# Masked copies of v made by four DMAs within SBUF, pooled residual on GpSimd, and a TensorE loop that begins with the convolution

## Chip, core and metric

One core of one Trainium2 chip. The metric is the device time of the whole program in microseconds, the median of several runs.

## What is computed

`x` is 4 x 128 x 96 x 96 in f32. It is group-normalised (32 groups of 4 channels) and goes through a windowed linear attention over windows of 4 x 4 pixels; the result is added to `x`.

```python
qkv = jnp.einsum('nchw,oc->nohw', xw, qkv_w)        # xw: windows of the normalised x
pooled = _avg_pool5(qkv)                            # 5x5 mean, zero padding, within a window
msq = jnp.concatenate([qkv, pooled], axis=1)
msq = msq.reshape(N, -1, 3 * DIM, ws * ws).transpose(0, 1, 3, 2)
q = jax.nn.relu(msq[..., :DIM])
k = jax.nn.relu(msq[..., DIM:2 * DIM])
v = msq[..., 2 * DIM:]
v = jnp.pad(v, ((0, 0), (0, 0), (0, 0), (0, 1)), constant_values=1.0)
kv = jnp.einsum('ngld,nglm->ngdm', k, v)
out = jnp.einsum('ngld,ngdm->nglm', q, kv)
out = out[..., :-1] / (out[..., -1:] + 1e-15)
y = jnp.einsum('nchw,oc->nohw', out, proj_w)        # after going back to image order
y = y * inv[None, :, None, None] + (bn_beta - bn_mean * inv)[None, :, None, None]
x = x + y
```

## The kernel before

**Tiling.** All of `x` stays in SBUF (`x_all`, channels on the partitions). A strip is four image rows, 384 pixels, 24 windows; there are 96 strips (`NS`), 24 per image. Each strip goes through every stage twice: in full (16 pixels per window) and pooled (a 5x5 mean within a 4x4 window has only 9 different values, so 216 columns per strip).

**GpSimd (POOL)**, lines 226 to 279: `normalise_and_pool(s, p)` writes the normalised strip in window order to `xn[:, p]` (L255 subtracts the mean, L256 multiplies by the inverse deviation, signal `xn_ready`) and eight adds through the helper at L234 make the pooled sums `xp[:, p]` (`xp_ready`). Strip s+2 is made in step s, once TensorE has done `conv_q(s)` (semaphore `q_p`), which frees the buffer.

**TensorE (PE)**, lines 528 to 669. One step of the loop is, in this order: `kv_products` full, `kv_products` pooled (both L582, small 64x32 tiles of the array), `conv_q` (L556 full, L558 pooled), `conv_kv` of the next strip (L538, pixels stationary), `transposes` of the last strip's output (L627), `conv_kv_pooled` of the next strip (L549), `project` of the last strip (L633, L635), `out_products` full and pooled (both L611, small tiles). Step 0 and step 95 are written out; steps 1 to 94 are a hardware loop (`pe.Fori`) of 47 turns with two steps in its body. The program begins each step with `kv_products`, so the jump back lies between the pooled `out_products` and the full `kv_products`.

**ScalarE (ACT)**, lines 281 to 364. A step is `relu_q`, `relu_q_pooled`, `relu_k(s+1)` (L286), `to_image(s-1)` (L325), `pooled_out(s-1)` (L332), `masked_v(s+1)` full (L305, four copies of v, each scaled by a column of 0 and 1 so that only one window's rows are left), `relu_k_pooled(s+1)` (L292), `masked_v(s+1)` pooled (L305, six copies).

**VectorE (DVE)**, lines 366 to 526. A step is `own_heads` full and pooled (L446), the statistics of a later image in some steps (L377), `residual(s-1)` (L452 adds the full part of y and the shift to `x_all`; L462, four adds, spreads the pooled y over the 16 pixels of each window; signal `y_done`), `divide` full and pooled (L472, L473, L476). The pooled `kv_products` waits for `vm_p`, the last of the six pooled masks; the full `kv_products` for `km_f`, `vm_f` and `y_done`.

**SyncE (SP)** issues the loads and, for each strip, waits for `y_done` and issues the store (L222).

Of the kernel before, what the change touches and what calls it, by code (L numbers as in the profile page):

```python
# [8 lines left out]
ALU = mybir.AluOpType  # L9
ACT = mybir.ActivationFunctionType  # L10

P = 128
# [23 lines left out]
C_VF = C_OWN + QG * KC  # L36
C_VP = C_VF + EF
# [5 lines left out]
def constants():  # L43


    c = np.zeros((P, N_CONST), np.float32)
    p = np.arange(P)
    c[:, C_IDENT:C_IDENT + P] = np.eye(P)
    quad, head = p // Q4, p % Q4 // D
    for j in range(QG):  # L50
        at = C_OWN + j * KC
        c[:, at:at + KC] = (quad[:, None] % QG == j) & (head[:, None] == np.arange(KC)[None] // HC)
    win_f, win_p = p % Q4 // PX, p % Q4 // PXP
    side = np.array([1, 2, 1])
    times = (side[:, None] * side[None]).ravel()[p % Q4 % PXP][:, None]
    own_f = (quad % QG * WF + win_f)[:, None] == np.arange(EF)[None]
    own_p = ((quad % QG * WP + win_p)[:, None] == np.arange(EP)[None]) & (win_p < WP)[:, None]
    c[:, C_VF:C_VF + EF] = own_f
    c[:, C_VP:C_VP + EP] = own_p * times / 25.0
    c[:, C_TP:C_TP + EP] = own_p * times  # L60
    pads = p % Q4 >= WP * PXP
    c[np.concatenate([p[~pads], p[pads]]), C_PACK + p] = 1
    return c


def build(nc, x, wq, wkv, proj, bn, consts, out):
# [20 lines left out]
    with ExitStack() as ctx:  # L87
# [29 lines left out]
        xn = sb("xn", [2, SP])  # L117
        hs = sb("hs", [NW, WS, NP])
# [5 lines left out]
        vm_full = sb("vm_full", [TF, EF, 4, KC])  # L124
        vm_pool = sb("vm_pool", [TP, EP, 4, KC])
# [8 lines left out]
        o_sb = sb("o_sb", [SP + SPP])  # L134

# [33 lines left out]
        vm_f, vm_p = sem("vm_f"), sem("vm_p")  # L169
        qm_f, qm_p = sem("qm_f"), sem("qm_p")  # L170
# [7 lines left out]
        added_f = sem("added_f")  # L178
        y_done = sem("y_done")
# [30 lines left out]
        def _(sp):  # L210
# [7 lines left out]
            for b in range(B):  # L218
                for t in range(SPB):

                    sp.wait_ge(y_done, t + (b * SPB + 2))
                    sp.dma_start(out_v[:, b, bass.ds(t * SP, SP)],  # L222
                                 x_all[:, bass.ds(t * SP + b * HW, SP)]).then_inc(stored, 16)
# [3 lines left out]
        def _(pool):  # L227
# [3 lines left out]
            pool.memset(q_pool[:], 0.0).then_inc(pads_zero, 1)  # L231

# [3 lines left out]
            def normalise_and_pool(s, p):  # L236


                xr = xn[:, p].rearrange("p (w r c) -> p r w c", r=WS, c=WS)
                xv = xn[:, p].rearrange("p (w r c) -> p w r c", r=WS, c=WS)  # L240
                xo = xp[:, p].rearrange("p (q j) -> p q j", j=Q4)[:, :, 0:WP * PXP].rearrange(
                    "p q (w r c) -> p q w r c", w=WP, c=NP)
                h3 = hs[:].rearrange("p (q w) r c -> p q w r c", w=WP)
# [8 lines left out]
                src = x_all[:, bass.ds(s * SP, SP)].rearrange("p (r w c) -> p r w c", r=WS, c=WS)  # L252
# [6 lines left out]
                link(add(ht[:], xv[:, :, :, 1], xv[:, :, :, 2]), 2)  # L259
                link(add(hs[:, :, :, 0], ht[:], xv[:, :, :, 0]), 3)  # L260
                add(hs[:, :, :, 2], ht[:], xv[:, :, :, 3])
                link(add(hs[:, :, :, 1], hs[:, :, :, 0], xv[:, :, :, 3]), 4)
# [3 lines left out]
                add(xo[:, :, :, 1, :], xo[:, :, :, 0, :], h3[:, :, :, 3, :]).then_inc(xp_ready, 1)  # L266

            def step(s, b, at, phase):
                if s < NS - 2:
# [3 lines left out]
                    normalise_and_pool(s + 2, s % 2)  # L273

            pool.wait_ge(pads_zero, 3)
# [3 lines left out]
            over_strips(step)  # L279

        @block.scalar
        def _(act):
# [12 lines left out]
            def masked_v(s, pooled):  # L295

                ready, free, done, bank, vm, tiles, wins, mask = (
                    (v_p, kv_p, vm_p, V_P, vm_pool, TP, EP, C_VP) if pooled else
                    (v_f, kv_f, vm_f, V_F, vm_full, TF, EF, C_VF))
                act.wait_ge(ready, s + 1)  # L300
                wait(act, free, s)
                heads = vm[:].rearrange("p t e i (h c) -> p t e (i h) c", c=HC)
                src = ps[:, bank, 0:tiles * P].rearrange("p (t h m) -> p t h m", t=tiles, m=D)
                for e in range(wins):
                    last = act.activation(heads[:, :, e, :, 0:D], src, ACT.Copy, scale=col(mask + e))  # L305
                last.then_inc(done, 1)
# [26 lines left out]

            def square_root(n):
# [6 lines left out]
            act.wait_ge(pads_zero, 3)  # L341

            def step(s, b, at, phase):
                relu_q(s)
                relu_q_pooled(s)
                if not is_last(s):
                    relu_k(s + 1)
                if not is_first(s):
                    to_image(s - 1)
                    pooled_out(s - 1)  # L350
                if not is_last(s):
                    masked_v(s + 1, False)
                    relu_k_pooled(s + 1)
                    masked_v(s + 1, True)
# [4 lines left out]
            masked_v(0, False)  # L359
            relu_k_pooled(0)  # L360
            masked_v(0, True)
            over_strips(step)
            to_image(NS - 1)
            pooled_out(NS - 1)

        @block.vector
        def _(dve):
# [48 lines left out]

            dve.memset(dev[:], 0.0).then_inc(y_done, 1)
# [31 lines left out]
            def residual(s):  # L449
# [4 lines left out]
                dve.wait_ge(y_p, s + 1)  # L454
                dve.wait_ge(added_f, s + 1)
                src = ps[:, Y_P, 0:SPP].rearrange("p (w r c) -> p w r c", r=NP, c=NP)
                dst = xs.rearrange("p (r w c) -> p w r c", r=WS, c=WS)
                ends, ends_p, mid, mid_p = slice(0, WS, WS - 1), slice(0, NP, NP - 1), slice(1, 3), slice(1, 2)
                for rows, rows_p in ((ends, ends_p), (mid, mid_p)):
                    for cols, cols_p in ((ends, ends_p), (mid, mid_p)):  # L460
                        part = dst[:, :, rows, cols]
                        last = dve.tensor_tensor(part, src[:, :, rows_p, cols_p].to_broadcast([P, NW, 2, 2]),  # L462
                                                 part, ALU.add)
                last.then_inc(y_done, 1)
# [53 lines left out]
            for vm, wins, mask in ((vm_full, EF, C_VF), (vm_pool, EP, C_TP)):  # L518
                for e in range(wins):
                    ones = vm[:, :, e].rearrange("p t i (h c) -> p t (i h) c", c=HC)[:, :, :, D]  # L520
                    last = dve.tensor_copy(ones, col(mask + e).unsqueeze(2).to_broadcast(list(ones.shape)))
# [7 lines left out]
        def _(pe):  # L529
# [12 lines left out]
            def conv_kv_pooled(s, p):  # L542
                pe.wait_ge(xp_ready, s + 1)

                wait(pe, qm_f, s)
# [16 lines left out]
            def kv_products(s, pooled):  # L562


                k, vm, tiles, wins, bank, done = (
                    (k_pool, vm_pool, TP, EP, KVP, kv_p) if pooled else (k_full, vm_full, TF, EF, KVF, kv_f))
                pe.wait_ge(km_p if pooled else km_f, s + 1)
                pe.wait_ge(vm_p if pooled else vm_f, s + 1)
                if pooled:

                    wait(pe, num_f, s)
                else:

                    wait(pe, y_done, s)

                pe.nop(nofuse=True)
                n = wins * KC
                for t in range(tiles):
                    for r in range(G):
                        rows = slice(H64 * r, H64 * (r + 1))  # L580
                        for i in range(4):
                            last = pe.matmul(ps[Q4 * i:Q4 * (i + 1), bank + r, t * n:(t + 1) * n],  # L582
                                             k[rows, t, Q4 * i:Q4 * (i + 1)], vm[rows, t, :, i, :],
                                             start=True, stop=True)
                last.then_inc(done, 1)

            def out_products(s, pooled):


                q, kvc, done, bank, tiles, wins = (  # L590
                    (q_pool, kvc_pool, out_p, OUTP, TP, WP) if pooled else
                    (q_full, kvc_full, out_f, OUTF, TF, WF))
                pe.wait_ge(qm_p if pooled else qm_f, s + 1)
                pe.wait_ge(kvc_p if pooled else kvc_f, s + 1)
                if not pooled:

                    pe.wait_ge(kvc_p, s + 1)
                elif not is_last(s):

                    pe.wait_ge(km_f, s + 2)  # L600
                    pe.wait_ge(vm_f, s + 2)
                pe.nop(nofuse=True)
                n = QG * KC
                blocks = q[:].rearrange("p n e j -> p n (e j)")
                for t in range(tiles):
                    for e in range(wins):
                        for g in range(G):
                            rows = slice(H64 * g, H64 * (g + 1))
# [88 lines left out]
```

## Time and profile before

| | us |
|---|---|
| median of 3 runs | 930.72 (928.78 to 931.36) |
| the profiled execution's own time | 930.24 |
| its span, first to last instruction | 928.3 |
| TensorE matmul busy | 873.8 |
| weight load busy | 733.4 |
| VectorE busy | 772.3 |
| ScalarE busy | 609.5 |
| GpSimd busy | 456.0 |
| mean granted TensorE clock | 0.993 of full speed |

Busy time is the union of an engine's instructions. The ends of matmuls are modelled, so on TensorE the distance from one start to the next says more than the busy time. "issue" as a releaser means that the engine waited for nothing that the profile shows.

### The profile page before, as it was taken

The numbers are of one execution on the slowest core, as the hardware profiler recorded it, in microseconds if no ns is written. First come the engines' busy times: TensorE is split into PE (matmuls) and PEld (weight loads), VectorE is DVE, ScalarE is ACT, GpSimd is POOL, SyncE is SP. The second block draws the span as 40 slices with busy tenths as digits, with TensorE's granted clock in tenths as the row PEclk, the third lists the DMA queues.
The fourth block names the chain that finished last, engine by engine and source line by source line (L and its number), as shares of the span: only waits on it lengthen the run. The fifth ranks groups of instructions, "written<-read, shape, count | busy, mean of one in ns | idle before, by whom it ended". The sixth has DMA issues, their size and how long they took to land.

```text
span 928.3 us, 65376 instructions
## 1 busy us (share of the span) xinstructions
PE 873.8 (94%) x29282; PEld 733.4 (79%) x29282; DVE 772.3 (83%) x1625; ACT 609.5 (66%) x1542; POOL 456.0 (49%) x967
## 2 busy tenths in 40 slices
PE   0689999999999999999999999999999999999997
PEld 0578888888888888888888888888888888888885
DVE  7369989998878898998878998999887878787886
ACT  0457676767676767676766667676767676767673
POOL 1545454545454545555554545454545454545550
PEclk9999999999999999999999999999999999999998
DMA  9910000000000000000000000000000000000000
GB/s 378 431 50 17 26 17 26 17 26 17 25 19 25 26 17 26 17 26 17 26 17 26 18 26 17 26 17 27 17 26 17 25 25 18 26 17 26 18 26 27
DMA packets 15893, 38.77 MB, mean 42 GB/s; under 512 B 1888, under 2 KB 14688, under 8 KB 15456
## 3 DMA queue, kind: packets, MB, share of 16 engines
q1 hardware_dynamic: 15840, 38.26, 10.6%
q14 instruction: 44, 0.36, 0.1%
q8 instruction: 9, 0.15, 0.1%
HBM read 19.38 MB, written 18.87 MB: 41 GB/s over the span
## 4 chain that ended last, share of the span: by engine, by line
PE 93%; issue 3%; DVE 2%; POOL 1%; DMA 0%; ACT 0%; DVEq 0%; POOLq 0%
PE ps L611 23%; PE ps L582 19%; PE ps L538 14%; PE ps L549 9%; PE ps L556 9%; PE ps L633 7%; PE ps L627 6%; PE ps L635 4%; PE ps L558 4%; DVE stats L377 1%; DMA x_all<-x 0%; POOL hs L234 0%; DVE kvc_full L446 0%; POOL xp L234 0%; ACT o_sb L325 0%
## 5 line engine op out<-in xcount | busy, mean ns | idle before, releaser
L255 POOL TENSOR_TENSOR xn<-x_all,mean_t 128x384 f32<-128x384 f32 x96 | 79.4, 827 | 393.6 <-PE ps L558 375.1
L305 ACT ACTIVATE vm_pool<-ps,cst 128x256 f32<-128x256 f32 x576 | 225.5, 543 | 0.4 <-PE ps L549 0.4
L446 DVE TENSOR_TENSOR kvc_full<-ps,cst 128x864 f32<-128x864 f32 x192 | 193.7, 1050 | 17.8 <-PE ps L582 17.6
L446 DVE TENSOR_TENSOR kvc_pool<-ps,cst 128x864 f32<-128x864 f32 x192 | 193.2, 1048 | 0.0
L305 ACT ACTIVATE vm_full<-ps,cst 128x384 f32<-128x384 f32 x384 | 192.2, 598 | 0.9 <-PE ps L538 0.9
L312 ACT ACTIVATE q_full<-ps 128x384 f32<-128x384 f32 x96 | 47.2, 491 | 208.5 <-PE ps L556 208.5
L538 PE MATMUL ps<-wkv_sb,xn 128*128 128x128 f32 x1152 | 145.5, 276 | 23.5 <-POOL xn L256 23.5
L538 PEld LDWEIGHTS ps<-wkv_sb,xn 128*128 128x128 f32 x1152 | 144.1, 193 | 23.5 <-issue 23.5
L452 DVE SCALAR_TENSOR_TENSOR x_all<-ps,shift,x_all 128x384 f32<-128x384 f32 x96 | 59.3, 618 | 93.4 <-PE ps L633 93.2
L611 PEld LDWEIGHTS ps<-kvc_full,q_full 64*32 64x32 f32 x9216 | 99.5, 105 | 26.4 <-issue 26.3
L611 PE MATMUL ps<-kvc_pool,q_pool 64*32 64x72 f32 x9216 | 115.8, 230 | 2.1 <-issue 2.1
L611 PE MATMUL ps<-kvc_full,q_full 64*32 64x72 f32 x9216 | 116.5, 230 | 0.9 <-issue 0.9
L582 PE MATMUL ps<-vm_full,k_full 64*32 64x144 f32 x4608 | 95.8, 289 | 21.5 <-issue 20.7
L611 PEld LDWEIGHTS ps<-kvc_pool,q_pool 64*32 64x32 f32 x9216 | 101.5, 105 | 6.7 <-issue 2.4
L549 PE MATMUL ps<-wkv_sb,xp 128*128 128x128 f32 x768 | 102.5, 277 | 0.6 <-POOL xp L234 0.6
L549 PEld LDWEIGHTS ps<-wkv_sb,xp 128*128 128x128 f32 x768 | 94.1, 193 | 0.9 <-POOL xp L234 0.9
L582 PE MATMUL ps<-vm_pool,k_pool 64*32 64x216 f32 x3072 | 94.1, 350 | 0.3
L582 PEld LDWEIGHTS ps<-vm_full,k_full 64*32 64x32 f32 x4608 | 69.5, 106 | 31.5 <-issue 29.2
L234 POOL TENSOR_TENSOR hs<-ht,xn 128x96 f32<-128x96 f32 x192 | 85.6, 446 | 15.1
L556 PE MATMUL ps<-xn,wq_sb 128*128 128x384 f32 x192 | 88.4, 542 | 0.0
L256 POOL TENSOR_TENSOR xn<-xn,rstd_t 128x384 f32<-128x384 f32 x96 | 79.6, 829 | 7.6
L325 ACT ACTIVATE o_sb<-ps 128x384 f32<-128x384 f32 x96 | 47.2, 491 | 53.2 <-PE ps L627 53.2
(66 smaller groups left out, 1242.2 us busy)
## 6 DMA issues: line engine op xcount, KB each, us to landing
out<-x_all SPq DMA_DIRECT2D x96, 192.0 KB, 1.9
x_all<-x SPq DMA_DIRECT2D x3, 4608.0 KB, 32.1
x_all<-x SPq DMA_DIRECT2D x6, 768.0 KB, 8.1
cst<-consts SPq DMA_DIRECT2D x1, 172.0 KB, 11.0
wkv_sb<-wkv SPq DMA_DIRECT2D x1, 128.0 KB, 10.8
o_sb<-proj SPq DMA_DIRECT2D x1, 128.0 KB, 10.4
wq_sb<-wq SPq DMA_DIRECT2D x1, 64.0 KB, 10.5
bn_sb<-bn SPq DMA_DIRECT2D x1, 2.0 KB, 10.3
```

What stands on the lines that cost most here:

```text
L234: return pool.tensor_tensor(o, a, b, ALU.add)
L255: link(pool.tensor_tensor(xr, src, mean, ALU.subtract), 1)
L256: pool.tensor_tensor(xn[:, p], xn[:, p], rstd, ALU.mult).then_inc(xn_ready, 1)
L305: last = act.activation(heads[:, :, e, :, 0:D], src, ACT.Copy, scale=col(mask + e))
L446: last = dve.tensor_tensor(kvc[:, g], src.to_broadcast(shape), own, ALU.mult)
L452: dve.scalar_tensor_tensor(xs, ps[:, Y_F, 0:SP], shift[:], xs, ALU.add, ALU.add).then_inc(added_f, 1)
L538: last = pe.matmul(ps[:, bank, t * P:(t + 1) * P], xn[:, p, t * P:(t + 1) * P], wkv_sb[:, half * P:(half + 1) * P], start=True, stop=True)
L549: last = pe.matmul(ps[:, bank, t * P:(t + 1) * P], xp[:, p, t * P:(t + 1) * P], wkv_sb[:, half * P:(half + 1) * P], start=True, stop=True)
L556: pe.matmul(ps[:, Q_F, 0:SP], wq_sb[:], xn[:, p], start=True, stop=True).then_inc(q_f, 1)
L582: last = pe.matmul(ps[Q4 * i:Q4 * (i + 1), bank + r, t * n:(t + 1) * n], k[rows, t, Q4 * i:Q4 * (i + 1)], vm[rows, t, :, i, :], start=True ...
L611: last = pe.matmul(ps[Q4 * c:Q4 * (c + 1), bank + g, t * n:(t + 1) * n], blocks[rows, 4 * t + c, Q4 * e:Q4 * (e + 1)], kvc[rows, r, w], st ...
L633: pe.matmul(ps[:, Y_F, 0:SP], projT[:, 0:P], o_sb[:, 0:SP], start=True, stop=True).then_inc(y_f, 1)
```

## The change

- The mask columns `C_VF` go, and the normalised strip is stored with the pixels of four windows interleaved: in every group of 64 stationary pixels, row 4n+e belongs to window e.
- ScalarE makes one copy of v per strip (`copy_v`, 128x384, into `v_full`, whose ninth column is set to one beforehand) instead of the four masked ones. SyncE then issues four DMAs per strip within SBUF (`spread_v`), the e-th from the rows e, e+4, ... of `v_full` into the same rows of window e of `vm_full`, whose other rows were set to zero at the start. `kv_products` waits for all four.
- `conv_q` reads `xn` in window order, that is with a step of four f32 (16 bytes) from one column to the next.
- GpSimd multiplies by the inverse deviation in four instructions, and takes over the four pooled adds (`residual_pooled`); since it reads SBUF, ScalarE first copies the pooled y out of PSUM (`copy_y_pooled`).
- TensorE's step is rotated: it begins with `conv_kv(s+1)` and ends with `kv_products(s+1)` and `conv_q(s+1)`. The order of the stages around the loop is as before. The pooled v copies no longer stand between `conv_q`'s two matmuls as a wait, and several other waits that another one implies are gone.

```diff
...
+            def spread_v(s):
+                sp.wait_ge(v_copied, s + 1)
+                wait(sp, kv_f, s)
+                for e in range(EF):
+                    rows = slice(e, P, EF)
+                    sp.dma_start(vm_full[rows, :, e], v_full[rows]).then_inc(vm_f, 16)
+            def store(s):
+                sp.wait_ge(y_done, s + 1)
+                sp.dma_start(out_v[:, s // SPB, s % SPB * SP:(s % SPB + 1) * SP],
+                             x_all[:, s * SP:(s + 1) * SP]).then_inc(stored, 16)
+            spread_v(0)
+            for s in range(NS):
+                if not is_last(s):
+                    spread_v(s + 1)
+                if not is_first(s):
+                    store(s - 1)
+            store(NS - 1)
...
-                xr = xn[:, p].rearrange("p (w r c) -> p r w c", r=WS, c=WS)
-                xv = xn[:, p].rearrange("p (w r c) -> p w r c", r=WS, c=WS)
+                xr = xn[:, p].rearrange("p (g r c e) -> p r g e c", r=WS, c=WS, e=EF)
+                xv = xn[:, p].rearrange("p (g r c e) -> p c g e r", r=WS, c=WS, e=EF)
...
-                mean = mean_t[:, bass.ds(s, 1)].unsqueeze(2).unsqueeze(3).to_broadcast([P, WS, NW, WS])
-                rstd = rstd_t[:, bass.ds(s, 1)].to_broadcast([P, SP])
-                link(pool.tensor_tensor(xr, src, mean, ALU.subtract), 1)
-                pool.tensor_tensor(xn[:, p], xn[:, p], rstd, ALU.mult).then_inc(xn_ready, 1)
+                mean = mean_t[:, s:s + 1].to_broadcast([P, SP])
+                rstd = rstd_t[:, s:s + 1].unsqueeze(2).unsqueeze(3).to_broadcast([P, SP // WS // 16, EF, WS])
+                link(pool.tensor_tensor(xd[:], x_all[:, s * SP:(s + 1) * SP], mean, ALU.subtract), 1)
+                rows = xd[:].rearrange("p (r g e c) -> p r g e c", r=WS, e=EF, c=WS)
+                for r in range(WS):
+                    last = pool.tensor_tensor(xr[:, r], rows[:, r], rstd, ALU.mult)
+                last.then_inc(xn_ready, 1)
...
+            def residual_pooled(s):
+                pool.wait_ge(added_f, s + 1)
+                pool.wait_ge(y_copied, s + 1)
+                src = y_pool[:].rearrange("p (w r c) -> p w r c", r=NP, c=NP)
+                dst = x_all[:, s * SP:(s + 1) * SP].rearrange("p (r w c) -> p w r c", r=WS, c=WS)
+                ends, ends_p, mid, mid_p = slice(0, WS, WS - 1), slice(0, NP, NP - 1), slice(1, 3), slice(1, 2)
+                for rows, rows_p in ((ends, ends_p), (mid, mid_p)):
+                    for cols, cols_p in ((ends, ends_p), (mid, mid_p)):
+                        part = dst[:, :, rows, cols]
+                        last = add(part, src[:, :, rows_p, cols_p].to_broadcast([P, NW, 2, 2]), part)
+                last.then_inc(y_done, 1)
...
+            def copy_v(s):
+                act.wait_ge(v_f, s + 1)
+                wait(act, vm_f, 16 * EF * s)
+                act.activation(v_full[:].rearrange("p t (h c) -> p t h c", c=HC)[:, :, :, 0:D],
+                               ps[:, V_F, 0:TF * P].rearrange("p (t h m) -> p t h m", t=TF, m=D),
+                               ACT.Copy).then_inc(v_copied, 1)
+            def masked_v_pooled(s, between=None):
+                act.wait_ge(v_p, s + 1)
+                wait(act, kv_p, s)
+                heads = vm_pool[:].rearrange("p t e (h c) -> p t e h c", c=HC)
+                src = ps[:, V_P, 0:TP * P].rearrange("p (t h m) -> p t h m", t=TP, m=D)
+                for e in range(EP):
+                    last = act.activation(heads[:, :, e, :, 0:D], src, ACT.Copy, scale=col(C_VP + e))
+                    if between is not None and e == 1:
+                        copy_y_pooled(between)
+                last.then_inc(vm_p, 1)
...
+            def copy_y_pooled(s):
+                act.wait_ge(y_p, s + 1)
+                wait(act, y_done, s)
+                act.activation(y_pool[:], ps[:, Y_P, 0:SPP], ACT.Copy).then_inc(y_copied, 1)
...
             def step(s, b, at, phase):
                 relu_q(s)
                 relu_q_pooled(s)
                 if not is_last(s):
                     relu_k(s + 1)
+                    copy_v(s + 1)
                 if not is_first(s):
                     to_image(s - 1)
                     pooled_out(s - 1)
                 if not is_last(s):
-                    masked_v(s + 1, False)
                     relu_k_pooled(s + 1)
-                    masked_v(s + 1, True)
+                    masked_v_pooled(s + 1, None if is_first(s) else s - 1)
+                elif not is_first(s):
+                    copy_y_pooled(s - 1)
...
-                pe.wait_ge(km_p, s + 1)
-                pe.matmul(ps[:, Q_F, 0:SP], wq_sb[:], xn[:, p], start=True, stop=True).then_inc(q_f, 1)
-                pe.wait_ge(vm_p, s + 1)
+                pe.matmul(ps[:, Q_F, 0:SP], wq_sb[:], xn[:, p].rearrange("p (g j e) -> p g e j", j=PX, e=EF),
+                          start=True, stop=True).then_inc(q_f, 1)
                 pe.matmul(ps[:, Q_P, 0:SPP], wq_sb[:],
                           xp[:, p].rearrange("p (q j) -> p q j", j=Q4)[:, :, 0:WP * PXP],
...
+            def kv_products(s):
+                wait(pe, added_f, s - 1)
+                wait(pe, y_copied, s - 1)
+                pe.wait_ge(km_f, s + 1)
+                pe.wait_ge(vm_f, 16 * EF * (s + 1))
+                pe.nop(nofuse=True)
+                for t in range(TF):
+                    last = kv_tile(False, t)
+                last.then_inc(kv_f, 1)
+            def kv_products_pooled(s):
+                pe.wait_ge(vm_p, s + 1)
+                wait(pe, num_f, s)
+                pe.nop(nofuse=True)
+                for t in range(TP):
+                    last = kv_tile(True, t)
+                last.then_inc(kv_p, 1)
+            def out_products(s):
+                if is_last(s):
+                    pe.wait_ge(qm_p, s + 1)
+                pe.wait_ge(kvc_p, s + 1)
+                pe.nop(nofuse=True)
+                for t in range(TF):
+                    for e in range(WF):
+                        last = out_tile(False, t, e)
+                last.then_inc(out_f, 1)
+            def out_products_pooled(s):
+                if not is_last(s):
+                    pe.wait_ge(v_copied, s + 2)
+                    pe.nop(nofuse=True)
+                for t in range(TP):
+                    for e in range(WP):
+                        last = out_tile(True, t, e)
+                last.then_inc(out_p, 1)
 
...
             def step(s, p):
-                kv_products(s, False)
-                kv_products(s, True)
-                conv_q(s, p)
-                if not is_last(s):
-                    conv_kv(s + 1, 1 - p)
+                conv_kv(s + 1, p)
                 if not is_first(s):
                     transposes(s - 1)
-                if not is_last(s):
-                    conv_kv_pooled(s + 1, 1 - p)
+                conv_kv_pooled(s + 1, p)
                 if not is_first(s):
                     project(s - 1)
-                out_products(s, False)
-                out_products(s, True)
+                out_products(s)
+                out_products_pooled(s)
+                kv_products(s + 1)
+                kv_products_pooled(s + 1)
+                conv_q(s + 1, p)
             conv_kv(0, 0)
             conv_kv_pooled(0, 0)
@@ -659,12 +714,19 @@
             last.then_inc(proj_turned, 1)
             pe.wait_ge(projT_ready, 1)
             pe.wait_ge(ones_set, 1)
-            step(0, 0)
+            kv_products(0)
+            kv_products_pooled(0)
+            conv_q(0, 0)
+            step(0, 1)
             with pe.Fori(1, NS - 1, 2) as s:
-                step(s, 1)
-                step(s + 1, 0)
-            step(NS - 1, (NS - 1) % 2)
+                step(s, 0)
+                step(s + 1, 1)
+            transposes(NS - 2)
+            project(NS - 2)
+            out_products(NS - 1)
+            out_products_pooled(NS - 1)
             transposes(NS - 1)
             project(NS - 1)
...
```

## Rows read from the trace of the kernel before

**Rows 1.** The page, the chain that ended last, shares of the span.
```profile
PE 93%; issue 3%; DVE 2%; POOL 1%; DMA 0%; ACT 0%; DVEq 0%; POOLq 0%
```

**Rows 2.** The waits of the whole span (total us, times, longest).
```profile
PE ps L582 <- issue: 20.7, 47, 4.5
```

**Rows 3.** The timeline of TensorE's matmuls, 500 to 520 us (start us, us).
```profile
507.05 1.20 PE L611 MATMUL ps<-kvc_pool,q_pool 64*32 64x72 f32 x96
508.60 0.98 PE L582 MATMUL ps<-vm_full,k_full 64*32 64x144 f32 x48 [0.35 <-issue]
509.36 0.96 PE L582 MATMUL ps<-vm_pool,k_pool 64*32 64x216 f32 x32
510.26 0.91 PE L556 MATMUL ps<-xn,wq_sb 128*128 128x384 f32 x2
511.00 0.53 PE L558 MATMUL ps<-xp,wq_sb 128*128 128x216 f32 x2
511.37 1.50 PE L538 MATMUL ps<-wkv_sb,xn 128*128 128x128 f32 x12
...
514.15 0.81 PE L633 MATMUL ps<-o_sb,projT 128*128 128x384 f32 x2
514.79 0.53 PE L635 MATMUL ps<-o_sb,projT 128*128 128x216 f32 x2
...
516.36 1.20 PE L611 MATMUL ps<-kvc_pool,q_pool 64*32 64x72 f32 x96
517.46 0.98 PE L582 MATMUL ps<-vm_full,k_full 64*32 64x144 f32 x48
518.42 0.96 PE L582 MATMUL ps<-vm_pool,k_pool 64*32 64x216 f32 x32
519.32 0.91 PE L556 MATMUL ps<-xn,wq_sb 128*128 128x384 f32 x2
```

**Rows 4.** The timeline of ScalarE in the same stretch.
```profile
512.24 0.49 ACT L286 ACTIVATE k_full<-ps 128x384 f32<-128x384 f32 x1 [0.28 <-PE ps L538]
513.24 0.49 ACT L325 ACTIVATE o_sb<-ps 128x384 f32<-128x384 f32 x1 [0.51 <-PE ps L627]
513.62 0.34 ACT L332 ACTIVATE o_sb<-ps 128x216 f32<-128x216 f32 x1
513.85 2.00 ACT L305 ACTIVATE vm_full<-ps,cst 128x384 f32<-128x384 f32 x4
515.71 0.42 ACT L292 ACTIVATE k_pool<-ps 128x256 f32<-128x256 f32 x1
515.97 2.35 ACT L305 ACTIVATE vm_pool<-ps,cst 128x256 f32<-128x256 f32 x6
```

**Rows 5.** The timeline from the start: two DMA issues of SyncE.
```profile
4.40 0.45 SPq L215 DMA_DIRECT2D wkv_sb<-wkv  x1
4.89 0.45 SPq L215 DMA_DIRECT2D wq_sb<-wq  x1
```

**Rows 6.** The page's DMA issues (KB each, us from issue to landing).
```profile
out<-x_all SPq DMA_DIRECT2D x96, 192.0 KB, 1.9
```

**Rows 7.** The timeline of GpSimd, one strip's first and last instruction.
```profile
511.62 0.83 POOL L255 TENSOR_TENSOR xn<-x_all,mean_t 128x384 f32<-128x384 f32 x1 [4.03 <-PE ps L558]
...
516.52 0.36 POOL L234 TENSOR_TENSOR xp<-xp,hs 128x72 f32<-128x72 f32 x1
```

**Rows 8.** Groups of instructions by form (xcount | busy us, mean ns).
```profile
L462 DVE TENSOR_TENSOR x_all<-ps,x_all 128x96 f32<-128x96 f32 x384 | 72.5, 252 | 10.1
L234 POOL TENSOR_TENSOR hs<-hs,xn 128x96 f32<-128x96 f32 x96 | 49.6, 517 | 0.0
L234 POOL TENSOR_TENSOR ht<-xn 128x96 f32<-128x96 f32 x96 | 34.9, 363 | 7.5
```

**Rows 9.** The timeline of the first 50 us: the first strip's v and `kv_products`.
```profile
26.45 2.00 ACT L305 ACTIVATE vm_full<-ps,cst 128x384 f32<-128x384 f32 x4 [0.70 <-PE ps L538]
...
30.09 1.70 PE L582 MATMUL ps<-vm_full,k_full 64*32 64x144 f32 x48 [0.61 <-DVE projT L524]
```

More of the change, by code:

```diff
@@ L35 @@
 C_OWN = P
-C_VF = C_OWN + QG * KC
-C_VP = C_VF + EF
+C_VP = C_OWN + QG * KC
 C_TP = C_VP + EP
@@ L123, in build @@
         k_pool = sb("k_pool", [TP, P])
-        vm_full = sb("vm_full", [TF, EF, 4, KC])
-        vm_pool = sb("vm_pool", [TP, EP, 4, KC])
+        v_full = sb("v_full", [TF, 4 * KC])
+        vm_full = sb("vm_full", [TF, EF, 4 * KC])
+        vm_pool = sb("vm_pool", [TP, EP, 4 * KC])
         q_full = sb("q_full", [TF * 4, WF, Q4 + PX])
@@ L178, in build @@
         added_f = sem("added_f")
+        y_copied = sem("y_copied")
         y_done = sem("y_done")
@@ L251, in normalise_and_pool @@
                 wait(pool, q_p, s - 1)
[L252 to L256 removed]
+                mean = mean_t[:, s:s + 1].to_broadcast([P, SP])
[5 more added lines that the diff above has]
+                last.then_inc(xn_ready, 1)
                 pool.wait_ge(xn_ready, s + 1)
[L259 to L262, printed above, removed]
+                link(add(t4, xv[:, 1], xv[:, 2]), 2)
+                link(add(h4[:, 0], t4, xv[:, 0]), 3)
+                add(h4[:, 2], t4, xv[:, 3])
+                link(add(h4[:, 1], h4[:, 0], xv[:, 3]), 4)
                 link(add(vt[:], hs[:, :, 1, :], hs[:, :, 2, :]), 5)
@@ L273, in step @@
                     normalise_and_pool(s + 2, s % 2)
-            pool.wait_ge(pads_zero, 3)
+                if not is_first(s):
+                    residual_pooled(s - 1)
+            pool.wait_ge(pads_zero, 5)
             pool.wait_ge(dv_group, GS)
@@ L279, in _ @@
             over_strips(step)
+            residual_pooled(NS - 1)
         @block.scalar
@@ L293, in relu_k_pooled @@
                                ACT.Relu, scale=1 / 25.0).then_inc(km_p, 1)
[L295 to L306, printed above, removed]
+            def copy_v(s):
[14 more added lines that the diff above has]
+                last.then_inc(vm_p, 1)
             def relu_q(s):
@@ L358, in _ @@
             relu_k(0)
-            masked_v(0, False)
+            copy_v(0)
             relu_k_pooled(0)
-            masked_v(0, True)
+            masked_v_pooled(0)
             over_strips(step)
@@ L364, in _ @@
             pooled_out(NS - 1)
+            copy_y_pooled(NS - 1)
         @block.vector
@@ L453, in residual @@
                                          ALU.add).then_inc(added_f, 1)
[L454 to L464, printed above, removed]
             def divide(s, pooled):
@@ L516, in _ @@
             dve.tensor_scalar(proj_sb, proj_sb, bn_inv[:], None, ALU.mult).then_inc(proj_scaled, 1)
[L518 to L521, printed above, removed]
+            for e in range(EP):
+                ones = vm_pool[:, :, e].rearrange("p t (h c) -> p t h c", c=HC)[:, :, :, D]
+                last = dve.tensor_copy(ones, col(C_TP + e).unsqueeze(2).to_broadcast(list(ones.shape)))
             last.then_inc(ones_set, 1)
@@ L560, in conv_q @@
                           start=True, stop=True).then_inc(q_p, 1)
[L562 to L602, printed above, removed]
+            def kv_tile(pooled, t):
+                k, vm, bank, n = (k_pool, vm_pool, KVP, EP * KC) if pooled else (k_full, vm_full, KVF, EF * KC)
+                for r in range(G):
+                    rows = slice(H64 * r, H64 * (r + 1))
+                    for i in range(4):
+                        last = pe.matmul(ps[Q4 * i:Q4 * (i + 1), bank + r, t * n:(t + 1) * n],
+                                         k[rows, t, Q4 * i:Q4 * (i + 1)], vm[rows, t, :, i * KC:(i + 1) * KC],
+                                         start=True, stop=True)
+                return last
@@ L603, in out_products, with out_tile @@
+            def out_tile(pooled, t, e):
+                q, kvc, bank, wins = (q_pool, kvc_pool, OUTP, WP) if pooled else (q_full, kvc_full, OUTF, WF)
                 n = QG * KC
                 blocks = q[:].rearrange("p n e j -> p n (e j)")
[L605 to L608, printed above, removed]
-                            for c in range(4):
-                                r, w = c // QG, t * QG * wins + c % QG * wins + e
-                                last = pe.matmul(ps[Q4 * c:Q4 * (c + 1), bank + g, t * n:(t + 1) * n],
-                                                 blocks[rows, 4 * t + c, Q4 * e:Q4 * (e + 1)], kvc[rows, r, w],
-                                                 start=e == 0, stop=e == wins - 1)
@@ L614, in out_products @@
-                last.then_inc(done, 1)
+                for g in range(G):
+                    rows = slice(H64 * g, H64 * (g + 1))
+                    for c in range(4):
+                        r, w = c // QG, t * QG * wins + c % QG * wins + e
+                        last = pe.matmul(ps[Q4 * c:Q4 * (c + 1), bank + g, t * n:(t + 1) * n],
+                                         blocks[rows, 4 * t + c, Q4 * e:Q4 * (e + 1)], kvc[rows, r, w],
+                                         start=e == 0, stop=e == wins - 1)
@@ new lines, in out_tile @@
+                return last
+            def kv_products(s):
[14 more added lines that the diff above has]
+                last.then_inc(kv_p, 1)
@@ L622, in transposes @@
                 else:
-                    pe.wait_ge(y_done, s + 1)
+                    pe.wait_ge(num_p, s + 1)
+                    pe.wait_ge(added_f, s)
+                    pe.wait_ge(y_copied, s)
                 for bank, o, n, pxs, columns, done in (
```

22 lines of the change are left out of this document (9 added, 13 removed).

## The prediction

> **What bounds the kernel now.** I read the chain that ended last first: 93% of it is TensorE's own work, 3% "issue", nothing else above 2% [rows 1]. So an edit pays only where TensorE stands still, and the other engines matter only if they begin to hold it up. Next, the waits: the one idle entry of TensorE that recurs once per turn of its loop is "issue" ahead of L582, 20.7 us in 47 waits, the longest 4.5 [rows 2]. There are 47 turns of two strips each. Then the timeline of two successive steps, measured from start to start because the ends are modelled [rows 3].
>
> - From full `kv_products` to the next one, 508.60 to 517.46: **8.86 us**. I take this as the floor of a strip, since neither stall below falls in it.
> - From pooled `out_products` to the next one, 507.05 to 516.36: 9.31. The stage before the jump takes 508.60 - 507.05 = 1.55, the same stage one step later 517.46 - 516.36 = 1.10. The jump costs **0.45 us per turn**.
> - From pooled `kv_products` to the next one, 509.36 to 518.42: 9.06. The full stage before it takes 0.76 after the jump and 0.96 one step later: **0.20 us per turn**. The reader is to see why in ScalarE's rows: the six pooled masks run from 515.97 to 518.32, and the pooled `kv_products` starts at 518.42, 0.10 later [rows 3, 4]. It waits for `vm_p`. In the step with the jump that wait is hidden by the jump itself.
>
> So 0.65 us per turn is idle, 0.65 x 47 = 30.6 us over the loop; everything else of a step is matmuls at the higher of the clock's two levels (2.4 GHz, mean granted 0.993).
>
> **ScalarE.** The change takes out four instructions of 128x384 (2.00 us) and puts in one of 0.49 and one copy of 128x216 at 0.34 [rows 4]. What matters is when `vm_p` comes. On the times of [rows 4]: `relu_k` ends at 512.73. v is ready when `conv_kv`'s second half is through; the first half released `relu_k` at 512.24, half of the 12 matmuls that take 1.34 follow, so v comes at about 512.91. `copy_v` ends near 513.40; it stands in what was a wait of 0.51 for the transposes. `to_image` and `pooled_out` shift by 0.1 at most, to about 514.0. `relu_k_pooled` (0.42) ends near 514.4, two masks (2.35 / 6 = 0.39 each) end near 515.2, then `copy_y_pooled` has to wait for the pooled projection, started at 514.79 with 0.53 and a delivery of 0.1 to 0.2 [rows 3], so about 515.45 to 515.8, and the other four masks end near **517.4**. Before, it was 518.32. In a step of 8.86 the pooled `kv_products` wants it at 517.46 + 0.76 = 518.2. Slack 0.8: the 0.20 goes, and `copy_y_pooled`, the new wait with four masks queued behind it, stays hidden. Gain 0.20 x 47 = **9.4 us**.
>
> **The rotated loop.** The same stages in the same cyclic order, but the jump now follows `conv_q`. Before it, TensorE has only small matmuls in hand (96 in 1.10 us); now it has `conv_q`, four large ones that fill 1.11 us (510.26 to 511.37), and the wait that stood between them is gone, so nothing stops the sequencer once the pooled `kv_products` has begun. The exposed part was 0.45; I take it as hidden entirely: 0.45 x 47 = **21.1 us**. Bounds: nothing hidden (0) and all of it. The 4.5 us once, at the loop's first entry, I leave as it is. The waits dropped ahead of other stages I cost at nothing, with this bound: `conv_q`'s full half takes 0.74 to the next start (510.26 to 511.00), the projection of equal size 0.64 (514.15 to 514.79), so the wait removed between its halves could be worth up to 0.10 x 96 = 9.6 us.
>
> **v by DMA.** New on the way to the full `kv_products`: v copied at 513.40, SyncE sees it near 513.5, and issues four DMAs. Two issues at the start lie 0.49 apart [rows 5], so the fourth starts at 513.5 + 3 x 0.49 = 514.97. The only price for landing is the store's 1.9 us for 192 KB [rows 6]; the copies are 54 KB each. I take 1.9: landed at 516.9, wanted at 517.46. Slack **0.6 us**, cost nothing. Bounds: below, the issue alone (landed at 515.5); above, pieces of 576 bytes that land in twice the time (518.8, 1.3 us late, every strip). The store of strip s-1 is queued on SyncE ahead of the DMAs of s+2, and waits for GpSimd: by the next part that is over about 2 us before those DMAs can start.
>
> **GpSimd.** Before, a strip takes from 511.62 to 516.88: 5.26 us [rows 7]. One multiply of 0.83 becomes four of 128x96, and four adds of 128x96 come in. The same form costs 0.363 (two strided inputs, packed output) to 0.517 (everything strided) [rows 8]; with some 0.04 between instructions, 0.40 to 0.56. I take 0.45 for the multiplies and 0.50 for the adds: 5.26 - 0.83 + 4 x 0.45 + 4 x 0.50 = **8.2 us**, bounds 7.6 and 8.9, against 8.86. Its waits (`added_f`, `y_copied`) are over near 515.9 and it gets there at 517.9. `xn` for strip s+2 comes 1 us later than before, but is wanted only a step later. Cost nothing while it stays under 8.86.
>
> **VectorE** loses four adds of 0.252 [rows 8]; it isn't on the chain, worth nothing, except at the end.
>
> **Start and end.** The first strip's v was ready at 26.45 + 2.00 = 28.45 and `kv_products` began at 30.09 for another reason [rows 9]. Now GpSimd's four multiplies add 1.0, and v needs 0.49 + 1.47 + 1.9 = 3.9 from 27.45: 31.3, so +1.2. At the end the pooled adds take 4 x 0.50 on GpSimd for 4 x 0.25 on VectorE, and a handover: +1.2. Together **+2.4**.
>
> **conv_q reading with a step of 16 bytes** is the cost that no row prices: all of TensorE's operands are packed now, and the trace's strided cases are GpSimd's, where the form goes from 0.363 to 0.517, a factor of 1.42 [rows 8]. I take nothing for the forecast, the lower bound, because an f32 column takes TensorE two cycles (384 columns in 0.32 us, half of 514.15 to 514.79) and a single element per cycle pair is little to fetch. The upper bound is a doubling, +0.64 per strip.
>
> **Sum**, against the profiled execution's own 930.24: - 21.1 - 9.4 + 2.4 = 902.1. The median of the runs is 930.72, 0.5 above it. I say **902 us**.
>
> **The rivals.**
>
> 1. **The strided read is slow** (20%, mostly slower than before). Mechanism: `conv_q` full, 96 times. A factor of 1.42 is 0.27 us per strip, 26 us: 928. Doubled it is 0.64, 61 us: 963. It decides from 28.1 / 96 = 0.29 us per strip up; middle 0.45, or 945 us. For it speaks GpSimd's factor of 1.42, against it only TensorE's low rate per column. The Trainium skill, Advanced Engine Details and Errata, section SBUF Cachelines, says that each access to a different 16-byte line pays and that two hits on a line are needed to hide the latency; by it every column of this read is such an access and this rival, not the forecast, would be the result. No TensorE row of this trace shows it.
> 2. **The jump isn't hidden**, only moved (12%): 902 + 21 = 923.
> 3. **v lands late** (7%): the slack of 0.6 is used up by slower small pieces or slower issues. At 2.9 us of landing v is 0.4 late in each strip, 38 us, 940. It decides from 2.8 us of landing up, where 0.3 late takes back the whole gain.
> 4. **GpSimd becomes the bound** (6%): if the 2x2 adds cost 0.75 each, a strip takes 9.2 us there, which is the old mean of 9.19 (half of 18.37, 9.31 + 9.06): 932. It decides from 8.86 up.
>
> **Chances.** The forecast 55%. Faster than before by over 0.3% (2.8 us, about what a measurement of this kernel tells from no change): 0.55 + 0.12 and 0.03 from the mild ends of the others, 0.70. Within: 0.07. Slower: 0.16 from rival 1, 0.07 from rivals 3 and 4, 0.23. **Range.** Low end: 902 less the 9.6 for the dropped wait, 892. High end 938: rivals 2 and 4 whole, the lower half of rival 1. What is left out is the upper part of rival 1 (about 0.11), of rival 3 (0.03) and a little below. The forecast's own range is 892 to 908.
>
> **What would show it.** Right: full `kv_products` to the next 8.9 us in every step; no "issue" of 0.35 once per turn; `vm_p` 0.8 ahead; TensorE's rows for `conv_q` full still 0.74 apart from the pooled half; SyncE's last v DMA landed half a microsecond before `kv_products`; GpSimd busy 85 to 95%. Wrong: `conv_q` full at 1.0 us or more to the next start; an idle of TensorE put down to a DMA ahead of `kv_products`, or to GpSimd ahead of `conv_kv`.

## The result and the profile after

| | before | after |
|---|---|---|
| median, us | 930.73 (928.78 to 931.36) | 990.35 (988.15 to 991.42) |
| the profiled execution's own time, us | 930.24 | 991.42 |
| its span, us | 928.3 | 989.6 |
| VectorE, ScalarE, GpSimd busy, us | 772.3, 609.5, 456.0 | 695.2, 509.2, 664.8 |

The ratio is 1.0641, 95% interval 1.0616 to 1.0667: **60 us slower**, where 28 us faster was forecast. It is the end of rival 1 (a doubled read), and something that no rival named. The page after:

```profile
PE 929.8 (94%) x29282; PEld 741.4 (75%) x29282; DVE 695.2 (70%) x1236; ACT 509.2 (51%) x1350; POOL 664.8 (67%) x1641
...
PE 93%; DMA 3%; DVE 2%; issue 1%; SPq 1%; ACT 0%; POOL 0%; POOLq 0%; DVEq 0%; ACTq 0%
```

The chain is TensorE's as before [rows 1], but 3% of it is now DMA. "issue" has gone from 3% to 1%. The busy time of TensorE grew by 56 us though it has the same 29282 matmuls, so one form of matmul must have become slower. The groups by form name it; the first row is of the kernel before:

```profile
L556 PE MATMUL ps<-xn,wq_sb 128*128 128x384 f32 x192 | 88.4, 542 | 0.0
```

and after:

```profile
L595 PE MATMUL ps<-xn,wq_sb 128*128 128x384 f32 x192 | 153.5, 889 | 0.0
L280 POOL TENSOR_TENSOR xn<-xd,rstd_t 128x96 f32<-128x96 f32 x384 | 122.6, 366 | 7.5
L255 POOL TENSOR_TENSOR x_all<-y_pool,x_all 128x96 f32<-128x96 f32 x384 | 150.4, 424 | 17.1 <-ACT y_pool L384 17.1
L339 ACT ACTIVATE v_full<-ps 128x384 f32<-128x384 f32 x96 | 47.2, 492 | 18.3 <-PE ps L579 18.3
```

The full half of `conv_q` alone takes 153.5 - 88.4 = 65 us more. The timeline of TensorE, one step, to be laid beside [rows 3]:

```profile
503.19 0.98 PE L608 MATMUL ps<-vm_full,k_full 64*32 64x144 f32 x48
503.92 0.98 PE L608 MATMUL ps<-vm_pool,k_pool 64*32 64x216 f32 x32
504.83 1.60 PE L595 MATMUL ps<-xn,wq_sb 128*128 128x384 f32 x2
506.25 0.55 PE L597 MATMUL ps<-xp,wq_sb 128*128 128x216 f32 x2
506.63 1.50 PE L579 MATMUL ps<-wkv_sb,xn 128*128 128x128 f32 x12
...
511.51 1.27 PE L623 MATMUL ps<-kvc_pool,q_pool 64*32 64x72 f32 x96
512.78 0.98 PE L608 MATMUL ps<-vm_full,k_full 64*32 64x144 f32 x48
```

`conv_q` full to the pooled half is 1.42 instead of 0.74. A strip takes 512.78 - 503.19 = 9.59 (the median of all strips is 9.60): the two stalls of before are gone, and 0.68 has come. The second finding stands in the waits of the whole span:

```profile
PE ps L608 <- DMA vm_full<-v_full: 21.5, 3, 20.9
```

One wait of 20.9 us. The timeline of the start shows where:

```profile
27.19 2.61 SPq L228 DMA_DIRECT2D vm_full<-v_full  x4
...
50.78 1.66 PE L608 MATMUL ps<-vm_full,k_full 64*32 64x144 f32 x43 [20.94 <-DMA vm_full<-v_full]
```

The first four copies of v are issued at 27.2; a DMA raises a semaphore when its data has landed, and by these events in the trace the last of the four lands at 50.5, 21.3 us after its issue. They stand in SyncE's queue behind three loads of 4.6 MB each. The trace's DMA packets, all of one queue, show the order: the first packet of 576 bytes (v) starts at 47.75, together with the last one of the loads.

### The profile page after: what moved, and what is told of

It is laid out like the page before. It is cut to its first block, busy times and chain, and to the rows that moved or that the text cites. A ratio compares the mean times of both kernels' runs of the same rounds, so it can differ in the third digit from the quotient of the medians.

```text
span 989.6 us, 65754 instructions
## 1 busy us (share of the span) xinstructions
PE 929.8 (94%) x29282; PEld 741.4 (75%) x29282; DVE 695.2 (70%) x1236; ACT 509.2 (51%) x1350; POOL 664.8 (67%) x1641
## 4 chain that ended last, share of the span: by engine, by line
PE 93%; DMA 3%; DVE 2%; issue 1%; SPq 1%; ACT 0%; POOL 0%; POOLq 0%; DVEq 0%; ACTq 0%
PE ps L623 21%; PE ps L608 17%; PE ps L595 15%; PE ps L579 13%; PE ps L589 8%; PE ps L689 6%; PE ps L683 5%; PE ps L597 4%; PE ps L691 3%; DMA vm_full<-v_full 3%; DVE stats L432 1%; SPq L228 1%; DMA x_all<-x 0%; ACT v_full L339 0%; POOL xn L280 0%
## 5 line engine op out<-in xcount | busy, mean ns | idle before, releaser
L277 POOL TENSOR_TENSOR xd<-x_all,mean_t 128x384 f32<-128x384 f32 x96 | 79.3, 826 | 252.1 <-PE ps L597 235.7
L350 ACT ACTIVATE vm_pool<-ps,cst 128x256 f32<-128x256 f32 x576 | 230.4, 478 | 5.1 <-PE ps L589 0.5
L255 POOL TENSOR_TENSOR x_all<-y_pool,x_all 128x96 f32<-128x96 f32 x384 | 150.4, 424 | 17.1 <-ACT y_pool L384 17.1
L595 PE MATMUL ps<-xn,wq_sb 128*128 128x384 f32 x192 | 153.5, 889 | 0.0
L280 POOL TENSOR_TENSOR xn<-xd,rstd_t 128x96 f32<-128x96 f32 x384 | 122.6, 366 | 7.5
L623 PE MATMUL ps<-kvc_pool,q_pool 64*32 64x72 f32 x9216 | 122.4, 232 | 2.9 <-issue 2.9
L623 PEld LDWEIGHTS ps<-kvc_pool,q_pool 64*32 64x32 f32 x9216 | 108.0, 105 | 3.4 <-issue 3.3
L597 PEld LDWEIGHTS ps<-xp,wq_sb 128*128 128x128 f32 x192 | 40.3, 210 | 87.8 <-issue 87.8
```

The lines of the kernel that those rows point to most:

```text
L255: return pool.tensor_tensor(o, a, b, ALU.add)
L277: link(pool.tensor_tensor(xd[:], x_all[:, s * SP:(s + 1) * SP], mean, ALU.subtract), 1)
L280: last = pool.tensor_tensor(xr[:, r], rows[:, r], rstd, ALU.mult)
L595: pe.matmul(ps[:, Q_F, 0:SP], wq_sb[:], xn[:, p].rearrange("p (g j e) -> p g e j", j=PX, e=EF), start=True, stop=True).then_inc(q_f, 1)
L597: pe.matmul(ps[:, Q_P, 0:SPP], wq_sb[:], xp[:, p].rearrange("p (q j) -> p q j", j=Q4)[:, :, 0:WP * PXP], start=True, stop=True).then_inc(q ...
L623: last = pe.matmul(ps[Q4 * c:Q4 * (c + 1), bank + g, t * n:(t + 1) * n], blocks[rows, 4 * t + c, Q4 * e:Q4 * (e + 1)], kvc[rows, r, w], st ...
```

## The experiments

All times are medians, unless a single run is named, beside the kernel before on the same chip (930.3, 930.8 and 930.0 us in the three groups).

**Without the strided read.** ScalarE reorders instead:

```diff
-pe.matmul(ps[:, Q_F, 0:SP], wq_sb[:], xn[:, p].rearrange("p (g j e) -> p g e j", j=PX, e=EF), ...
+pe.matmul(ps[:, Q_F, 0:SP], wq_sb[:], xn[:, p], ...
-act.activation(q_full[:, :, :, 0:PX], ps[:, Q_F, 0:SP].rearrange("p (n e j) -> p n e j", e=WF, j=PX),
+blocks = q_full[:].rearrange("p n e j -> p (n e) j").rearrange("p (g w) j -> p g w j", w=EF)
+act.activation(blocks[:, :, :, 0:PX], ps[:, Q_F, 0:SP].rearrange("p (g j w) -> p g w j", j=PX, w=EF),
```

> The changed kernel, with conv_q's full half reading xn packed (columns in the order in which they lie) and ScalarE's relu_q doing the reordering when it reads PSUM. Theory: the step of 16 bytes doubles TensorE's time for these 384 columns, 0.74 to 1.42 us per strip; without it 0.68 x 96 = 65 us go, 990 to about 925. But then the strip (9.59 - 0.68 = 8.91) is held by the way of v through the DMAs, not by TensorE. Rival (the lengthening comes from elsewhere in conv_q, such as waits or the neighbours): the time stays above 980. If ScalarE pays for the strided read of PSUM, relu_q is longer than 0.49.

Measured 923.95, ratio 0.9931 (0.9911 to 0.995): 66 us of the lengthening go with this edit. ScalarE's strided read of PSUM costs it nothing, 492 ns against 490:

```profile
L360 ACT ACTIVATE q_full<-ps 128x384 f32<-128x384 f32 x96 | 47.3, 492 | 311.2 <-PE ps L597 311.2
```

**Loads out of the way.** The loads of images 3 and 4 go strip by strip, and VectorE waits for each where it needs it.

```diff
-for b in range(1, B):
-    sp.dma_start(x_all[:, b * HW:(b + 1) * HW], x_v[:, b]).then_inc(loaded_batch[b - 1], 16)
+sp.dma_start(x_all[:, HW:2 * HW], x_v[:, 1]).then_inc(loaded_batch[0], 16)
...
+                if s + 2 * SPB < NS:
+                    load(s + 2 * SPB)      # one strip, behind spread_v(s + 1) and store(s - 1)
```

> The changed kernel, with the loads of images 3 and 4 no longer issued at the start but one strip per step, behind that step's v copies. Theory: the first strip's v copies stood behind 14 MB of loads in the same queue (TensorE idle 20.9 us ahead of its first kv_products); this gives about 20 us, 990 to 970. Rival (the first v copies are slow for another reason, such as a first use of this kind of transfer): no gain. The extra issue per step costs SyncE 0.35 to 0.5 us, which is hidden.

Measured 971.42, 18.9 us less than the changed kernel. The first `kv_products` starts at 31.27 instead of 50.78, and the last of the first four copies lands 1.87 us after its issue, so they aren't slow by being the first of their kind. TensorE's waits for these DMAs fall to 2.6 us in all:

```profile
PE ps L615 <- DMA vm_full<-v_full: 2.6, 4, 1.5
```

No run puts the v copies on another queue, so it stays open how much of the 20 us is the order in the queue and how much is that the loads keep the DMA engines busy.

**Both.**

> Both edits together. Theory: 990 - 65 - 20 = 905, with a strip of 8.91 us set by conv_kv, copy of v, four issues, landing, kv_products. Rival (the prediction's floor for TensorE, 8.86, or less, is reached): 900 or below.

Measured 903.81, ratio 0.9721 (0.97 to 0.9742). With the two costs taken out the kernel stands 2 us from the 902 forecast, and the strip is 8.90 (502.76 to 511.66):

```profile
502.76 0.98 PE L617 MATMUL ps<-vm_full,k_full 64*32 64x144 f32 x48
...
510.40 1.26 PE L632 MATMUL ps<-kvc_pool,q_pool 64*32 64x72 f32 x96
511.66 0.98 PE L617 MATMUL ps<-vm_full,k_full 64*32 64x144 f32 x48
```

That it comes so near is partly luck, as the runs with v earlier show below: v is late here, which costs 9 us, and the rest is 7 us better than forecast.

**The read alone, in the kernel before**, with steps of 4, 3 and 2 elements (`"p (g j e) -> p g e j"` with e=4; `"p (j e) -> p e j"` with e=3 and e=2).

> The kernel before, with conv_q's full half reading xn with a step of 4 f32 (16 bytes) and nothing else changed (the columns of q come in another order, so the output is another one). Theory: the read alone costs 0.68 per strip here too, 931 to 996. Rival (the read costs only together with GpSimd's or the DMAs' new traffic): below 940.

> The same with a step of 3 f32 (12 bytes). Between the two: three of four columns begin a new 16-byte line; 0.74 if only a step of 16 bytes or more costs, about 1.2 to 1.4 if each new line does.

> The kernel before, with conv_q's full half reading xn with a step of 2 f32 (8 bytes); columns of q in another order. If the price goes by steps that leave a 16-byte line at every column, this one costs nothing or little (0.74 to the next start); if any step other than one element costs, it is 1.42 here too, 996 us.

Measured 994.6, 963.69 and 931.03 us, the last two in a single run each. The columns of q come in another order in these three kernels, so they compute another result; the work is the same. The rows of `conv_q` full, in this order, a fence for each kernel:

```profile
L556 PE MATMUL ps<-xn,wq_sb 128*128 128x384 f32 x192 | 153.6, 889 | 0.0
```

```profile
L556 PE MATMUL ps<-xn,wq_sb 128*128 128x384 f32 x192 | 122.3, 722 | 0.0
```

```profile
L556 PE MATMUL ps<-xn,wq_sb 128*128 128x384 f32 x192 | 90.8, 554 | 0.0
```

To the start of the pooled half, in the same order:

```profile
515.09 1.60 PE L556 MATMUL ps<-xn,wq_sb 128*128 128x384 f32 x2
516.51 0.55 PE L558 MATMUL ps<-xp,wq_sb 128*128 128x216 f32 x2
```

```profile
509.74 1.27 PE L556 MATMUL ps<-xn,wq_sb 128*128 128x384 f32 x2
510.84 0.54 PE L558 MATMUL ps<-xp,wq_sb 128*128 128x216 f32 x2
```

```profile
500.99 0.94 PE L556 MATMUL ps<-xn,wq_sb 128*128 128x384 f32 x2
501.77 0.53 PE L558 MATMUL ps<-xp,wq_sb 128*128 128x216 f32 x2
```

It is 1.42, 1.10 and 0.78 us, against 0.74 packed. The price is the read's own: no GpSimd or DMA work was added here. It fits how often a new 16-byte line begins: a step of 2 elements begins 192 lines for 384 columns and is nearly free, 3 begins 288, 4 begins 384. If a line costs as much as two columns, the 0.64 of 384 packed columns becomes 0.64, 0.96 and 1.28; measured, it rose by 0.04, 0.36 and 0.68, that is by 0.04 more than this in each. No run took a step above 16 bytes, so the runs don't show whether the price stops there, as a price per line would, or goes on with the bytes stepped over.

The Trainium skill (Advanced Engine Details and Errata, SBUF Cachelines) has the rule of 16-byte lines with two hits needed on each; the three runs agree with it for TensorE's moving f32 operand.

**Is v late?** Two ways to bring it earlier, alone and together. First, v ahead of k on TensorE and ScalarE (and `out_products_pooled` waits for `km_f` instead of `v_copied`, since `relu_k` is now the last reader of the banks):

```diff
-for half, bank, done in ((0, K_F, k_f), (1, V_F, v_f)):
+for half, bank, done in ((1, V_F, v_f), (0, K_F, k_f)):
...
-relu_k(s + 1); copy_v(s + 1)
+copy_v(s + 1); relu_k(s + 1)
```

> a3_both, with v's half of conv_kv ahead of k's and ScalarE's copy of v ahead of relu_k, so that v is copied about 0.65 us earlier. Theory (the DMAs of v land too late: a strip of a3_both is 8.90 and the pooled out_products, 1.26 us to the next start, hold a wait of 0.16 for them): the wait goes, 0.16 x 95 = 15 us, 904 to 889. Rival (those 1.26 are TensorE's own work in this order of the loop): stays at 904.

Measured 894.82, ratio 0.9611 (0.9595 to 0.9627), 9 us below the one with both edits, not 15. The pooled `out_products` went from 1.26 to 1.20 to the next start, and the strip is 8.83:

```profile
513.51 1.20 PE L632 MATMUL ps<-kvc_pool,q_pool 64*32 64x72 f32 x96
514.71 0.98 PE L617 MATMUL ps<-vm_full,k_full 64*32 64x144 f32 x48
```

So v was late by 0.06 to 0.09 per strip, less than I had read from 1.26 - 1.10: of these 0.16, 0.10 is TensorE's own, and the full `out_products` takes 1.00 instead of 1.11. The semaphore events agree: with both edits `kv_products` starts 0.27 us after the last copy has landed (median), about as soon as in the first strip, where it surely waits for it (0.25); with v first it starts 0.88 after it. Second, one piece of 1728 bytes per row:

```diff
-vm_full = sb("vm_full", [TF, EF, 4 * KC])
+vm_full = sb("vm_full", [EF, TF, 4 * KC])
-sp.dma_start(vm_full[rows, :, e], v_full[rows])
+sp.dma_start(vm_full[rows, e], v_full[rows])
```

> a3_both, with vm_full laid out window by window, so that each row of a v copy is one piece of 1728 bytes instead of three of 576. Theory: the issue (0.63 us each in a3_both, 96 pieces) becomes as short as the store's (0.34 to 0.45, 32 pieces), so the last of four starts 0.5 to 0.8 earlier and the wait of 0.16 goes: 904 to 889. Rival (the issue doesn't depend on the pieces): 0.63 stays and so does the time.

Measured 907.6: a miss. Four issues take 2.37 us instead of 2.52, so the pieces hardly matter to the issue, and the strip is 8.96. The wait for v did go: the pooled `out_products` takes 1.20, and the last copy has landed 0.48 before `kv_products`. But here the full `out_products` takes 1.12 to the next start and not 1.00, which is more than was won; I have no cause for it.

```profile
510.13 2.37 SPq L232 DMA_DIRECT2D vm_full<-v_full  x4
...
511.96 1.33 PE L634 MATMUL ps<-kvc_full,q_full 64*32 64x72 f32 x96
513.08 1.20 PE L634 MATMUL ps<-kvc_pool,q_pool 64*32 64x72 f32 x96
```

> Both ways of a4_v_first and a5_rows together. Theory: each one alone is enough to bring the DMAs' landing ahead of kv_products, so no more than the better of the two (889); TensorE's own work is then the bound, about 8.74 per strip. Rival (the DMAs are later than that wait shows): faster than both by another 5 us or more.

Measured 894.22, ratio 0.9617 (0.96 to 0.9634), the same as with v first alone. TensorE's work, 8.84 a strip, is the bound: v has landed 1.07 before `kv_products` starts. This and the one before it are the fastest versions, 36 us below the kernel before.

**The jump.** The last version with the loop turned back:

```diff
 def step(s, p):
+    kv_products(s)
+    kv_products_pooled(s)
+    conv_q(s, p)
-    conv_kv(s + 1, p)
+    conv_kv(s + 1, 1 - p)
     ...
-    kv_products(s + 1)
-    kv_products_pooled(s + 1)
-    conv_q(s + 1, p)
```

> a6_rows_v_first, with TensorE's loop beginning with kv_products again, as in the kernel before. Theory (the jump costs 0.45 us per turn where only small matmuls are in hand and nothing behind conv_q): 0.45 x 47 = 21 us slower than a6_rows_v_first, 889 to 910. Rival (the rotation hides nothing by itself, the waits that went with it did): the same time as a6_rows_v_first.

Measured 918.91: 24.7 us, 0.53 per turn. The gap is back at its old place, once per two steps:

```profile
515.99 1.20 PE L634 MATMUL ps<-kvc_pool,q_pool 64*32 64x72 f32 x96
517.73 0.98 PE L619 MATMUL ps<-vm_full,k_full 64*32 64x144 f32 x48 [0.54 <-issue]
```

**The rotation alone, in the kernel before** (the same edit the other way round).

> The kernel before, with TensorE's loop rotated and nothing else (all masks, waits and adds as they were). Theory: the jump's 0.45 per turn is hidden behind conv_q, but then the wait for the pooled masks, which it covered in every second step, shows in both: each step 9.06, so 0.25 x 47 = 12 us, 930 to 918. Rival (ScalarE wasn't late, the 0.20 was something else): 8.86 in each step, 900. Rival (the rotation does nothing without the waits that went): 930.

Measured 920.32, ratio 0.9902 (0.9877 to 0.9927). Each step is 9.06, 504.92 to 513.98, and the pooled `kv_products` starts at 514.94, 0.10 after ScalarE's last mask:

```profile
504.92 0.98 PE L582 MATMUL ps<-vm_full,k_full 64*32 64x144 f32 x48
...
513.98 0.98 PE L582 MATMUL ps<-vm_full,k_full 64*32 64x144 f32 x48
514.94 0.96 PE L582 MATMUL ps<-vm_pool,k_pool 64*32 64x216 f32 x32
```

```profile
512.49 2.35 ACT L305 ACTIVATE vm_pool<-ps,cst 128x256 f32<-128x256 f32 x6
```

**The pooled residual back on VectorE** (`residual` with its four adds out of PSUM again, no `copy_y_pooled`).

> a6_rows_v_first, with the pooled residual on VectorE again, straight out of PSUM, and no copy of the pooled y. Theory: moving it to GpSimd was worth nothing in the loop (VectorE isn't on the chain) and costs about 1 us at the end: 894 to 893. Rival (VectorE's four adds delay its divide, and with it the stages after): slower than a6_rows_v_first by 5 us or more.

Measured 898.24, ratio 0.9663 (0.9641 to 0.9685): 4 us slower, between the two. An ordinary strip is 8.84 as well. Three times, once per later image, VectorE also does the group statistics and TensorE's `kv_products` comes to wait for its adds; the strip from 182.22 to 191.90, counted between two pooled `conv_q`, is 9.7 long. The three times make some 2.6 of the 4 us; for the rest I have no cause.

```profile
PE ps L604 <- DVE x_all L497: 1.6, 3, 0.5
```

## Why the prediction was wrong

**The step that failed** is "conv_q reading with a step of 16 bytes": "I take nothing for the forecast, the lower bound, because an f32 column takes TensorE two cycles ... and a single element per cycle pair is little to fetch". No row of the trace stood behind that; it was an argument from the rate. The run with the read alone shows the upper bound, 0.68 per strip, 65 us. The rival's doubling, 0.64 per strip, was right in size and in mechanism, and the chance of 20% for that rival was too low.

**The term that was missing** is the queue at the start. Under "Start and end" I priced the first v copies at 1.9 us of landing, the price of a store in the quiet middle of the run, and put `kv_products` at 31.3. It came at 50.78, behind loads that the page shows with 32 us to landing. The reader should take from it that a DMA's price depends on what is already under way or queued when it is issued. With the loads moved it came at 31.27, where I had put it.

**The other terms.**
- The floor of a strip, 8.86: measured 8.83 and 8.84 when nothing else limits.
- The jump, 0.45 per turn and hidden by `conv_q`: held, 0.53 in the kernel where only this was turned back.
- ScalarE's masks, 0.20 per turn: the rotation alone gave 10 us and left 9.06 in both steps, as this reading demands, and the rest came with the masks gone. So the forecast's two terms, 21.1 and 9.4, aren't each what one edit alone brings: the jump hid the wait for the masks in every second step. Only their sum is to be compared, and a strip fell from 9.19 on average to 8.84.
- The waits dropped ahead of other stages, up to 9.6: worth nothing, `conv_q` full takes 0.75 to the next start with packed reads.
- GpSimd, forecast 8.2 per strip: measured 7.4 (506.94 to 514.37, from its first instruction to its last of a strip); its adds cost 424 ns and its multiplies 366 instead of 450 to 500. No bound, and the edit is worth 4 us, not nothing, most of it because VectorE is short of time in three strips.
- v by DMA, slack forecast 0.6: it was late by some 0.08. `copy_v` starts where I had put it, 1.54 after `conv_kv`, and SyncE issues 0.03 after its end instead of 0.1. But the issues lie 0.64 apart, not 0.49 (the price of a load at the start), which takes 0.45 of the slack; and I had priced the landing and not the way from there to the matmul. The landing takes the 1.9 that I had taken for it (1.89, median, by the semaphore events), and `kv_products` starts 0.28 later. Together 0.59 + 0.07 - 0.45 - 0.28 = -0.07: from `conv_kv` to `kv_products` it is 6.15 (506.63 to 512.78), and 6.08 where v comes earlier. Small terms ate a slack that I had called enough; 9 us.

```profile
508.17 0.49 ACT L339 ACTIVATE v_full<-ps 128x384 f32<-128x384 f32 x1 [0.18 <-PE ps L579]
```

```profile
508.68 2.52 SPq L228 DMA_DIRECT2D vm_full<-v_full  x4
```

**The account.** The full `kv_products` of the first and the last strip cut the span in three. The first comes at 50.78 instead of 30.09: +20.7, where I had +1.2; 18.9 of it went with the loads. From the first to the last it is 922.75 instead of 882.57 us: +40.2, where I had -30.5. Read +65.3 and v late +6.7 (0.07 x 95) on top of my -30.5 make +41.5, so the middle is accounted for to within 1.3. Behind the last it is +0.4, where I had +1.2. Together +61.3; the executions' own times differ by 991.42 - 930.24 = 61.2.

## What to carry to other kernels

An f32 operand that TensorE streams should be packed, or step by at most two elements; put the reordering into the PSUM read of ScalarE, where it cost nothing here. Before work that every step waits for is moved to DMAs, price the distance of the issues and the way from landing to the waiting engine, look at what the queue holds when the first of them is issued, and spread large loads over the steps behind them. A hardware loop's jump should follow large matmuls with no wait between them and it: the same stages in the same order were 25 us faster here.

## What the runs showed beyond expectation

- An issue of SyncE costs 0.34 us for a store, and takes 0.64 from one to the next for a copy within SBUF of 96 pieces and 0.59 for one of 32 pieces: it hardly goes by the pieces.
- GpSimd's `ht` add, of the same size, rose from 363 to 557 ns when its inputs' innermost step went from 16 to 64 bytes. The step alone isn't shown to be the cause: the `hs` adds, which read one such input beside another tile, stayed where they were (446 before, 440 after; and 517, 513).

```profile
L255 POOL TENSOR_TENSOR ht<-xn 128x96 f32<-128x96 f32 x96 | 53.5, 557 | 7.5
...
L255 POOL TENSOR_TENSOR hs<-ht,xn 128x96 f32<-128x96 f32 x192 | 84.5, 440 | 15.1
```

- A 16-byte step on the written side cost GpSimd nothing visible: its multiplies of 128x96 took 366 ns, as the `ht` add of before with packed output did (363). The two forms also differ in how they read, so this is a comparison and no proof.
